# DLRM tower: one-hot lookups as plain fp32 matmuls, and a later wait ahead of the gathers of two batch tiles

## What is computed

```python
e = stack([tbl_f[ids[:, f]] for f in range(26)], axis=1)        # 512 x 26 x 128
combined = concatenate([dense[:, None, :], e], axis=1)          # 512 x 27 x 128
inter = einsum('bfd,bgd->bfg', combined, combined)[:, iu, ju]   # 351 pairs per sample
h = concatenate([dense, inter, dense], axis=1)                  # 512 x 607
h = maximum(h @ W_top1 + b_top1, 0)                             # 607 x 512
h = maximum(h @ W_top2 + b_top2, 0)                             # 512 x 256
y = h @ W_top3                                                  # 256 x 1
```

## Time and profile before

| | |
|---|---|
| median of three runs | 156.84 us |
| the profiled execution | 156.5 us |
| its span, first to last instruction | 154.7 us |
| mean granted TensorE clock over the span | 0.901 of 2.4 GHz |
| TensorE matmul busy | 117.9 us |
| VectorE, ScalarE busy | 74.1, 73.0 us |
| GpSimd busy, nearly all of it gathers | 68.4 us |

### The profile page before, as it was taken

How to read it: one execution, slowest core, us unless ns; L and a number is a source line. 1 busy time by engine, 2 the same in 40 slices (tenths; PEclk the granted TensorE clock), 3 DMA queues, 4 the chain that set the end, 5 groups by cost and what they waited for, 6 DMA issues and landing times.

```text
span 154.7 us, 2685 instructions
## 1 busy us (share of the span) xinstructions
PE 117.9 (76%) x1038; PEld 98.9 (64%) x1038; DVE 74.1 (48%) x153; ACT 73.0 (47%) x160; POOL 68.4 (44%) x75
## 2 busy tenths in 40 slices
PE   0689999985979967550595728489929989799994
PEld 0446776662756856540394628478829989798993
DVE  3499999999999960407204510030505020237000
ACT  6795994995897820426104522002505313236211
POOL 2648072260345747474447465446456474100000
PEclk9999999999999999776559997865985799999999
DMA  5828765487961011111112121111121111100000
GB/s 156 222 71 267 207 190 110 160 221 199 354 181 42 17 51 38 34 51 34 39 44 52 28 63 32 49 34 38 34 51 33 39 50 25 27 6 0 4 0 1
DMA packets 6304, 12.58 MB, mean 81 GB/s; under 512 B 2545, under 2 KB 3157, under 8 KB 6163
## 3 DMA queue, kind: packets, MB, share of 16 engines
q1 hardware_dynamic: 3971, 7.68, 17.2%
q0 software_dynamic: 2176, 4.46, 10.9%
q10 hardware_dynamic: 144, 0.26, 0.8%
HBM read 11.27 MB, written 0.00 MB: 73 GB/s over the span
## 4 chain that ended last, share of the span: by engine, by line
DMA 34%; PE 27%; POOL 24%; issue 13%; DVE 1%; ACT 1%
DMA rows<-in_tbl_dram,ids_i 31%; POOL rows L343 24%; PE ps L603 12%; PE ps L574 7%; PE ps L525 2%; PE ps L616 2%; DMA ids_i<-in_ids_dram 2%; PE ps L558 2%; DVE z L488 1%; PE ps L626 1%; PE ps L624 1%; ACT emb_t L403 0%; DVE h_t L497 0%; ACT y L430 0%
## 5 line engine op out<-in xcount | busy, mean ns | idle before, releaser
L343 POOL DMA_INDIRECT rows<-in_tbl_dram,ids_i x68 | 67.6, 994 | 63.0 <-DMA rows<-in_tbl_dram,ids_i 45.2
L461 DVE TENSOR_SCALAR hot<-ps,row_no 125x512 fp32r<-125x512 f32 x54 | 36.6, 739 | 1.0 <-PE ps L512 1.0
L488 DVE COPY z<-ps 32x112 f32<-32x112 f32 (+1 forms) x64 | 16.5, 258 | 34.9 <-PE ps L574 22.7
L574 PE MATMUL ps<-emb_t 128*64 128x52 f32 x512 | 23.6, 251 | 11.8 <-issue 8.3
L574 PEld LDWEIGHTS ps<-emb_t 128*64 128x64 f32 x512 | 21.1, 166 | 14.8 <-issue 11.3
L542 PE MATMUL ps<-hot,tab_hi 125*128 125x512 f32 x72 | 30.0, 416 | 0.8 <-issue 0.8
L411 ACT COPY z<-ps 32x112 f32<-32x112 f32 (+1 forms) x64 | 15.2, 238 | 30.8 <-PE ps L574 19.7
L545 PE MATMUL ps<-hot,tab_lo 125*128 125x512 f32 x72 | 29.1, 404 | 0.7 <-DVE tab_lo L450 0.7
L558 PE MATMUL ps<-ident,rows 128*128 128x128 f32 x68 | 12.0, 304 | 15.2 <-DMA rows<-in_tbl_dram,ids_i 9.7
L558 PEld LDWEIGHTS ps<-ident,rows 128*128 128x128 f32 x68 | 8.3, 153 | 18.3 <-DMA rows<-in_tbl_dram,ids_i 11.7
L542 PEld LDWEIGHTS ps<-hot,tab_hi 125*128 125x128 f32 x72 | 14.1, 196 | 5.5 <-issue 2.4
(11 more groups left out here) (44 smaller groups left out, 92.7 us busy)
## 6 DMA issues: line engine op xcount, KB each, us to landing
tab<-in_tbl_dram SPq DMA_DIRECT2D x9, 448.0 KB
rows<-in_tbl_dram,ids_i POOLq DMA_INDIRECT x68, 4.6
w_fold<-w_pair SPq DMA_DIRECT2D x1, 1024.0 KB
w<-in_W_top_dram SPq DMA_DIRECT2D x1, 512.0 KB, 5.1
tab<-in_tbl_dram SPq DMA_DIRECT2D x9, 52.0 KB
x_rows<-in_r_dense_features_dram ACTq DMA_DIRECT2D x1, 256.0 KB, 3.2
w_x<-in_W_top_dram SPq DMA_DIRECT2D x1, 256.0 KB
h_t<-in_W_top_dram SPq DMA_DIRECT2D x1, 256.0 KB
```

The source lines that it names most:

```text
L343: pool.indirect_dma_start(out=rows[:, t, gathered.index(f), :], out_offset=None, in_=tables[f - 1], in_offset=bass.IndirectOffsetOnAxis(id ...
L461: nc.vector.tensor_scalar(hot[0:RP, k % OHB], ps[0:RP, IDV + n % 2, :], row_no[0:RP, c:c + 1], None, ALU.is_equal).then_inc(hot_dve, 1)
L488: last = nc.vector.tensor_copy(dst, src)
L574: last = nc.tensor.matmul(ps[32 * q:32 * (q + GT), bank, col:col + GC], emb_t[:, t, b0:b0 + GT, :].rearrange("p b f -> p (b f)"), emb_t[:, ...
```

## The change

There are three parts.
- The table chunks and the one-hot columns are plain fp32, and one fp32 matmul takes the place of the two fp32r ones. `split_hi`, `split_lo`, `tab_hi`, `tab_lo` and their semaphores go. `tab` gets a third buffer, `hot` has 16. SP loads table n when the matmuls of table n - 3 are done. TensorE waits for the table's DMAs itself.
- `broadcast_ids(n + 2)` is issued before the last two chunks of table n, rather than behind them.
- GpSimd waits for the rows of the group before ahead of a group's second gather in tiles 0 and 1; in tiles 2 and 3 ahead of its first, as before.

```diff
-    OHB = 10
-    RAW = 2
-    SPLIT = 2
+    OHB = 16
+    RAW = 3
...
-        tab_hi = sb("tab_hi", [P, SPLIT, R8, D], F32R)
-        tab_lo = sb("tab_lo", [P, SPLIT, R8, D], F32R)
-        hot = sb("hot", [P, OHB, B], F32R)
+        hot = sb("hot", [P, OHB, B])
...
-                    sp.wait_ge(lo_ready, n - RAW + 1)
+                    sp.wait_ge(hot_used, (n - RAW + 1) * R8)
...
-                        if n == 0 and g:
-                            pool.wait_ge(rows_in[t][g - 1], 16 * sum(a > 0 for a in features(GROUPS[g - 1])))
-                        elif n == 0 and t:
-                            pool.wait_ge(rows_in[t - 1][NG - 1], 16 * len(features(GROUPS[NG - 1])))
+                        if n == (0 if t >= 2 else 1):
+                            if g:
+                                pool.wait_ge(rows_in[t][g - 1], 16 * sum(a > 0 for a in features(GROUPS[g - 1])))
+                            elif t:
+                                pool.wait_ge(rows_in[t - 1][NG - 1], 16 * len(features(GROUPS[NG - 1])))
...
-            def split_hi(n):
-                act.wait_ge(tab_in[n], 32)
-                if n >= SPLIT:
-                    act.wait_ge(hot_used, (n - SPLIT + 1) * R8)
-                nc.scalar.copy(tab_hi[0:RP, n % SPLIT], tab[0:RP, n % RAW]).then_inc(hi_ready, 1)
...
-            def split_lo(n):
-                dve.wait_ge(hi_ready, n + 1)
-                nc.vector.tensor_tensor(tab_lo[0:RP, n % SPLIT], tab[0:RP, n % RAW], tab_hi[0:RP, n % SPLIT].bitcast(F32),
-                                        ALU.subtract).then_inc(lo_ready, 1)
...
-                    pe.wait_ge(hi_ready, n + 1)
+                    pe.wait_ge(tab_in[n], 32)
                     bank = ps[:, ROT + bank_of(s), :]
                     for c in range(R8):
+                        if c == R8 - 2 and n + 2 < NH:
+                            broadcast_ids(n + 2)
...
-                        one_hot = hot[0:RP, (n * R8 + c) % OHB]
-                        nc.tensor.matmul(bank, tab_hi[0:RP, n % SPLIT, c], one_hot, start=c == 0, stop=False)
-                        if c == 0:
-                            pe.wait_ge(lo_ready, n + 1)
-                        nc.tensor.matmul(bank, tab_lo[0:RP, n % SPLIT, c], one_hot,
-                                         start=False, stop=c == R8 - 1).then_inc(hot_used, 1)
-                    if n + 2 < NH:
-                        broadcast_ids(n + 2)
+                        nc.tensor.matmul(bank, tab[0:RP, n % RAW, c], hot[0:RP, (n * R8 + c) % OHB],
+                                         start=c == 0, stop=c == R8 - 1).then_inc(hot_used, 1)
```

## The result

| | median, us | against the kernel before of the same series (95% interval) |
|---|---|---|
| changed kernel, the first comparison | 169.1 (before: 156.59) | 1.075 (1.048 to 1.101) |
| changed kernel again, second series below (`r_after`) | 167.5 (157.8) | 1.069 (1.053 to 1.086) |
| changed kernel again, third series, another chip (`r2_after`) | 155.9 (160.3) | 0.982 (0.971 to 0.994) |

A forecast was written before the change was run, and what follows sets the result against it. The gather chain over most of the length, and TensorE and VectorE in the tables, were taken as bounds. The tables add 29 us; row waits, half clock and gaps give back 17: 168 us, range 157 to 177.

The forecast's parts named there:

- The price of the fp32 matmul: TensorE's table chunks: one 512-column fp32 matmul costs 0.88 us, replacing two fp32r passes of 0.455 us together.
- The stage of the tables: TensorE's table lookups: 9.05 us each for tables 2 to 6, ending at 85.3; the stage grows by 29.2 us.
- Relieved engines are worth nothing: Table stage: dropping `tab_lo` and ScalarE's cast gains nothing, as those engines need 4 to 5 us a table, TensorE 9.05.
- The gathers: GpSimd, tiles 0 and 1: the moved wait takes 11.3 us off the gathers, worth nothing as they no longer bound.
- e2's rival B: Expectation for e2: the earlier gathers gave back part of the 17 us, so 3 to 8 us longer, 172 to 177.
- Behind the tables: From u0:0 at 86.7: TensorE's stretches taken over without row waits, g0:3 at 134.2, span 166.8 us.
- Rival 2: Behind the tables: not slower, all TensorE gaps go, 14.0 us less, 154.5; chance 0.18, whole or in part.
- 57.42 to 76.90: TensorE's stretch from u0:0 in the kernel before: forecast to stay whole, 19.5 us, to 106.2.
- 76.90 to 88.04: TensorE's next stretch, up to tile 0's first layer: forecast to stay at 11.1 us, to 117.3.

The follow-up runs named there:

- e3: Changed kernel with the spread of ids back behind each table's last chunk: 151.0 us in the first series, 151.3 in the third.
- e5: Changed kernel with one fp32r pass a chunk on the high halves, low halves left out: 150.9 us, 0.948 against the kernel before.
- e4: Changed kernel without any GpSimd wait between groups of gathers: 155.6 us, first series.
- e2: Changed kernel with GpSimd's wait back ahead of every group's first gather, first series: 156.2 us, 0.988 against the kernel before.
- r_fp32_only: The file of e2 again (changed kernel, GpSimd's waits as before), second series: 172.9 us, 1.102 against the kernel before.
- r2_before: The kernel before, unaltered, run again in the third series: 160.9 us.
- r_before: The kernel before, unaltered, run again in the second series: 157.9 us.
- e6: Kernel before (fp32r halves, ids behind the chunks) with GpSimd's wait behind a group's first gather in all four tiles: 134.4 us, 0.854, third series.

## Why the prediction was right, and where it was not

**The price of the fp32 matmul: right, a little high.** 0.88 us was taken between 0.853 and 0.91; measured are 0.864, two records of 0.432. This lies nearer to the 0.863 estimated from the Trainium skill's pages ("FP8 and Floating Point Precision", "TensorE Precision Notes", and "TensorE: Matmul & The Clock Gate", "Back-to-back issue gap") than to my value. I was too high by 0.016 a chunk, 1.2 us in all. A table still takes 9.11 us, since about 0.2 us more than counted go into the change-overs to the ids and from the store. Scaling a short matmul's record carried its fixed part along four times: four of 0.112 us are 0.448, one of 512 columns is 0.432. That makes the fixed part some 0.005 us a record, an estimate from these two rows.

**The stage of the tables: right.** Predicted: 9.05 us a table, first product at 86.7. Measured: 9.11 and 86.08. The wait for the store of the bank, which the move of the ids uncovers, is there in all five tables that were named for it: 0.67 or 0.68 us in four, 0.89 ahead of table 6, behind two transposes and not four. e3 turns the move back and gets that time back. e5 shows that the fp32 matmuls' time is the cause of the rest.

**Relieved engines are worth nothing: it fits, and no run tests it alone.** The casts and `tab_lo` are gone, and the stage is as long as TensorE's own work: VectorE is idle 5 us at a time for want of ids. That nothing of SP's is late also held: no wait for a table or for `w_fold` is in any of the fp32 traces.

**The gathers: right on a chip without gaps, half right on one with them.** TensorE never waits for rows. e4 agrees. The size was off: their last issue is at 124.49 in the first trace, 6.5 us earlier than 130.99 and not 11.3 (I had said 122 for the landing). I had expected fewer landings of 4 to 6 us beside the table loads, but GpSimd still waits 3 to 4.3 us for several landings up to 68 us. That cost nothing, as rows had slack. (The 2.5 us that the forecast took from issue to landing are 2.87 by its own, 0.94 + 1.93; nothing hangs on it.) But on the second chip the wait placed as before costs 5.4 us (172.9 against 167.5), where I had said that it costs nothing; e2's rival B, 3 to 8 us, came true here. Rows were there in time there too. In `r_fp32_only` the gaps went on to 128.1 and in `r_after` only to 112.2, and a copy to `z` started late, at 98.10 and not 93.56. That would fit with gathers that end sooner helping not by their rows but by what else goes on while they fly: the last goes out at 130.28 in the first of the two traces and at 121.52 in the other. It rests on one trace of each and isn't shown.

**Behind the tables: right for that comparison, for the stated reason only in part.** The steps, in the first trace and in `r2_after`:

| start of | predicted | first trace | r2_after |
|---|---|---|---|
| u0:0 | 86.7 | 86.1 | 87.2 |
| u0:1 | 106.2 | 101.4 | 96.9 |
| tile 0's first layer | 117.3 | 114.9 | 104.8 |
| g4:2 | 124.0 | 124.2 | 111.5 |
| u1:2 | 129.1 | 129.2 | 116.5 |
| g0:3 | 134.2 | 134.9 | 122.2 |
| span | 166.8 | 167.4 | 154.7 |

In the first trace the gaps recur in tiles 0 and 1 and not in tile 2, as forecast; u0:1 is 5 us early. From there to tile 0's first layer it takes 13.5 us and not 11.1, with gaps of 0.80 at 112.8 and 0.83 at 114.3, and from there to g4:2 9.3 and not 6.7. In that last stretch there is no gap: the first 16 records of line 579 take 3.23 us where `r2_after` has 1.95 (the granted clock was 0.57 from 114.8 to 118), and the second layer waits 1.06 us for `h_t`. I had counted it at full clock. The misses of 5 us early and 5 us late cancel, and that is luck.

**Rival 2 came true elsewhere.** "All gaps go, 154.5 us" had 0.18. `r2_after` is 155.9. Its condition was wrong: I had tied it to rows being there and the clock kept up. Where it came true its sizes were near: 57.42 to 76.90 was to shrink by 8.3 us and shrank by 9.8, 76.90 to 88.04 by 5.7 and 3.2. What decides comes with the series: its chip, its moment, or where the program and its data were placed, which these runs don't tell apart. The runs show this much: gaps are in all six traces of the first comparison and the second series, whether tables are fp32 or fp32r, and in none of the eight of the first and third series, in most of which gathers are in flight at the same steps. Three files, the kernel before, the changed kernel and e2, showed both. Neither the order of instructions nor gathers in flight is enough to bring them. What they wait for stays open; no view names it. The loading of the program's own code is a candidate that was not tested: the queue `q8 instruction` moved 8 packets, 0.13 MB, with gaps and without (`r_after`, `r2_after`), which settles nothing. That the first comparison had gaps, like the trace from which the forecast took them over, was not something that the forecast had a reason for.

**Why then does the kernel before hardly move?** Its medians are 156.6 and 157.8 us where there are gaps, 159.2 and 160.3 where there are none: it is no faster without them. It is paced by the chain of gathers. In `r2_before`, without gaps, TensorE waits for rows for 29.0 us. In `r_before`, with them, it is 8.9, and 8.4 pass in gaps of the products and transposes and 4.3 in a wait for a late copy. (The two traces are of executions of 161.8 and 154.5 us. The clock is no part of it: the mean granted one is higher with the gaps, 0.922 against 0.872.) So the gaps lie under the wait for rows and cost the kernel before little. The changed kernel has no wait for rows behind the tables, so there the gaps, with the late copies and the half clock that go with them, come through: 11.6 and 13.2 us between the medians. I had named the row waits as what is given back, and had not said that they were also the cover of the gaps. This account fits the traces here, but no run switches the gaps on or off, so it is argued and not shown.

**The whole sum.** Where there are no gaps, the change adds some 29 us to TensorE's work, and the kernel before has 29.0 us of waits for rows to give back, 26.0 of them behind the tables; the medians then differ by 4.4 us, the change being the lower. Nothing in these runs makes the two sizes alike; I take it for chance. Beside a kernel whose gathers are mostly out of the way the added work shows: 155.9 for the changed kernel and 134.4 for e6 in one series, 21.5 us, of which some 4 are the ids'. It is not the full 29; e6 still waits 6.2 us for rows.

## What to carry to other kernels

Price a matmul by its data type from a row of the same kernel: a plain fp32 matmul of 512 columns is one instruction and takes 0.864 us, two fp32r passes 0.455. Halving the count of instructions here nearly doubled the time.

A long wait on a chain covers what else goes wrong beneath it. Before the slower engine's work is put in its place, ask what that work was hiding. The cheapest gain here was to issue one gather ahead of the wait, in all tiles: some 1.3 us a group, 14.6% in all on a chip without gaps, and no other engine was touched.

When one file gives two times, compare kernels that ran side by side on one chip and look into the trace for the stage that differs, before any edit is held to account.

## What of the hardware had not been expected

- Gaps of TensorE up to 1.1 us with no releaser, between bursts of some five short matmuls, in some series and not in others: 11.9 us in `e5_hi_only` at the products alone, and in `r2_after` nothing but the 0.3 and 0.5 us that the other traces have too (lists of waits above). With them the copies of a finished product start late: in the earlier trace rows 3.9 us, in `r_after` 1.9 (93.56, for a product at 91.7), and in `r2_after` none, 0.11 us behind the product:

```profile
91.87 2.15 DVE L468 COPY z<-ps 32x112 f32<-32x112 f32 x8 [0.45 <-PE ps L550]
```

- In none of the traces is there such a gap behind the landing of the last gathered row, but for the waits of 0.3 us ahead of u0:2 (in e4) and of 0.5 us ahead of x2 just named. That fits with gathers being one of two conditions. It was not tested: the kernel without waits between gathers ran only on a chip that had no gaps.
